# Two-layer conditioned attention: the queries' exponentials of layer 1 taken head by head on ScalarE

## The chip, the cores and the metric

The kernel runs on one core of a Trainium2 chip. The metric is the device time of one execution in microseconds; the time before is the median of three runs. The profile is of one further execution on the same kind of core.

## The reference

Input is `x` of 32 sequences x 128 positions x 512 features, float32, and a condition vector of 1024 values per sequence. Two layers follow each other; each adds its result to its input.

Layer 0 has 16 heads of 32 features and ordinary softmax attention over the positions. Layer 1 has 8 heads of 64 features and linear attention, and the change is in it:

```
xn  = layer_norm(x)
q   = softmax(xn @ Wq + bq, over the 64 features of each head)
k   = softmax(xn @ Wk + bk + (1 - mask) * -1e6, over the 128 positions)
v   = (xn @ Wv + bv) * mask
att = k^T v            (64 x 64 per head)
y   = q att
h   = silu(layer_norm(y) * (1 + scale) + shift) @ W_out + b_out
out = x + h            (scale, shift: from silu(condition) @ W_emb + b_emb)
```

The softmax of the queries needs, for each position and head, the maximum over 64 features, the exponentials of the differences, and the inverse of their sum. The inverse is multiplied in later, when `y` is read.

## The kernel before

Everything is written by hand: five engine programs (PE, DVE, ACT, POOL, and SP for the DMAs) with a semaphore for each kind of operation. Each engine carries out its own list strictly in order, and waits where an operand or a buffer is not ready. A matrix product in float32 precision is made of three products of split operands (`three`, lines 1268 to 1270), hence the tiles `_hi` and `_lo`.

The 32 sequences are worked on in 16 pairs (`GROUP = 2`), and both layers go through `program` (line 254), a software pipeline. One call of `step1(n, f, k, late, slot)` handles three pairs at once: `n` is loaded, normalised and turned; `f` is projected to queries, keys and values; `k` is finished (attention, second normalisation, silu, output product); `late` is the second sequence of the pair before, whose output product and store come last. In full steps `k` runs from pair 0 to pair 13. In the step of pair 14 there is no `n`, in that of pair 15 neither `n` nor `f`. Between the second and the third call stands `film()`, which makes scale and shift from the condition. `b` is 0 or 1, the sequence in the pair.

The lists of layer 1 around the change, each in the engine's order:

- DVE (`step1`, line 1109): output(late,1), kv_out(k,0), key softmax, y_norm(k,0), kv_out(k,1), key softmax, v_add(f,0), y_norm(k,1), the statistics of `n`, film_scale(k,0), q_add(f,0), q_soft(f,0), silu(k,0), v_add(f,1), s_low_part(k,0), film_scale(k,1), k_sums(f), silu(k,1), q_add(f,1), s_low_part(k,1), q_soft(f,1), xt_low(n,0), xt_low(n,1), output(k,0), q_sums(f,0), q_sums(f,1).
- ACT (`step1`, line 770): kt_out(k,0), qt_out(k,0), kt_out(k,1), k_bias and k_exps, qt_out(k,1), k_bias and k_exps, tanh(k,0), q_exps(f,0), s_high(k,0), tanh(k,1), s_high(k,1), xt_high(n,0), xt_high(n,1), q_exps(f,1).
- POOL: residual(k,0), norm2(k,0), v_mask(f,0), norm2(k,1), add_shift(k,0), norm1(n,0), norm1(n,1) (these write `xn`), add_shift(k,1), v_mask(f,1), residual(k,1).
- PE (`step1`, line 1435): turn_k(k,0), turn_q(k,0), turn_k(k,1), output(late,1), key projection, turn_q(k,1), keys_values(k,0), key projection, query(k,0), keys_values(k,1), values, query(k,1), query projection, turn_yn(k,0), values, turn_yn(k,1), query projection, turn(n,0), output(k,0), turn(n,1). `claim` (line 1253) makes PE wait until the last reader of a PSUM bank has finished.

The second half of a sequence is one chain: film_scale (DVE, L981, writes `z_a`), add_shift (POOL, L537, `z_s`), tanh (ACT, L689, `th`), silu (DVE, L988, `th`), s_high (ACT, L694), s_low_part (DVE, L994), output (PE), output (DVE, L1000).

The queries: q_add (L1031) adds the bias into `q_tmp` (shown as `room` in the profile), one buffer for both sequences; q_soft takes the maximum of each head (L1036) and subtracts it into `q_exp` (L1040, also `room`); q_exps (L715) takes all 512 exponentials of a position in one instruction; q_sums adds up each head (L1047) and inverts (L1051) into `q_rec`. In `film()` of layer 1 the sums of the first pair are made.

Of the kernel before, what the change touches and what calls it, by code (L numbers as in the profile page):

```python
# [33 lines left out]
ALU = mybir.AluOpType  # L34
ACT = mybir.ActivationFunctionType
AX = mybir.AxisListType

P = 128
GROUP = 2
# [28 lines left out]
def done(stage, at):  # L68


    if at.reg is None and at.const < 0:
        return stage.always
    return stage.sem, (at + (1 + stage.earlier)).value()
# [10 lines left out]
def upto(stage, value):  # L84

    return stage.sem, stage.earlier + value


def build(nc, t, out):
# [9 lines left out]
             b=[t["L0_cond_q_b"], t["L0_cond_k_b"], t["L0_cond_v_b"], t["L0_cond_out_b"]],  # L99
# [4 lines left out]
             b=[t["L1_cond_bq"], t["L1_cond_bk"], t["L1_cond_bv"], t["L1_cond_b_out"]],  # L104
# [3 lines left out]
    H0, H1 = layers[0]["H"], layers[1]["H"]  # L108
    DH0, DH1 = D // H0, D // H1
# [6 lines left out]
    with ExitStack() as ctx:  # L116
        def sb(name, shape, dt=F32):
            return ctx.enter_context(nc.sbuf_tensor(name, shape, dt))
# [72 lines left out]
        q_exp = room[:, 0, :].rearrange("p (s b d) -> p s b d", s=2, b=GROUP)  # L191
        k_tmp = room[:, 2, 0:2 * D].rearrange("p (s d) -> p s d", s=2)
        q_tmp = room[:, 2, 2 * D:3 * D]
# [7 lines left out]
        q_max = sb("q_max", [P, H1])  # L201
        q_sum = sb("q_sum", [P, H1])
# [13 lines left out]
        def stages(names, earlier=0):  # L216
            return {n: Stage(sem(n), earlier) for n in names.split()}

        def counted_on(these, earlier):
# [15 lines left out]
                 "rec pt_pe0 pt_pe1 pt_pe2 pt_pe3 pt_out0 pt_out1 pt_out2 pt_out3 pv "  # L235
                 "pv_out")
        only1 = ("kt_pe qt_pe kt_out qt_out att_pe att_out kbias0 kbias1 kmax0 kmax1 ksub0 ksub1 kexp0 kexp1 ksum0 ksum1 krec "
                 "q_pe q_add qmax qsub qexp qsum qrec")
        both = stages(STAGES)

        moved = {n: [sem(f"{n}{b}") for b in range(GROUP)] for n in ("x_in_full", "res_in", "stored", "mask_row_in")}
# [349 lines left out]
        def _(act):  # L591
            act.wait_ge(consts, 1)
            for l, L in enumerate(layers):
                s, bk = S[l], BANKS[l]
# [115 lines left out]
                    act.activation(v, v, ACT.Exp).then_inc(s[f"kexp{pair}"].sem, GROUP)  # L710

                def q_exps(f, slot, b):
                    act.wait_ge(*done(s["qsub"], f + b))
                    v = q_exp[:, slot, b, :]
                    act.activation(v, v, ACT.Exp).then_inc(s["qexp"].sem, 1)  # L715

                def kt_out(k, b):
                    act.wait_ge(*done(s["kt_pe"], k + b))
# [86 lines left out]
        def _(dve):  # L805
            dve.wait_ge(consts, 1)
            for l, L in enumerate(layers):
                s, bk = S[l], BANKS[l]
# [83 lines left out]
                def film():  # L892

                    dve.wait_ge(*upto(s["emb_pe"], KE))
                    dve.tensor_tensor(yn[0:2 * B, 0, :], bank[bk["EMB"]][0:2 * B, :], x_out[0:2 * B, 0, :], ALU.add
                                      ).then_inc(s["emb_dve"].sem, 1)
                    dve.tensor_copy(yn[2 * B:4 * B, 0, :], bank[bk["EMB"]][2 * B:4 * B, :]).then_inc(s["emb_dve"].sem, 1)
                    if l == 1:
                        q_sums(At(None, 0), 0, 0)
                        q_sums(At(None, 0), 0, 1)  # L900
                    dve.wait_ge(*upto(s["film_pe"], 1))
                    et = z_s[:].rearrange("p a n -> p (a n)")[:, 0:2 * C * B].rearrange("p (c b) -> p c b", b=B)
                    fd = s["film_dve"]
                    dve.tensor_copy(et.rearrange("p c b -> p (c b)"), bank[bk["FILM"]][:, 0:2 * C * B]).then_inc(fd.sem, 1)
                    dve.wait_ge(*upto(fd, 1))
                    wide = lambda i: col[:, i, :].rearrange("p (c o) -> p c o", o=1).broadcast_to([P, C, B])
                    dve.scalar_tensor_tensor(out=film_a[:], in0=et[:, 0:C, :], scalar=1.0, in1=wide(W2),
                                             op0=ALU.add, op1=ALU.mult).then_inc(fd.sem, 1)
                    dve.scalar_tensor_tensor(out=film_b[:], in0=et[:, 0:C, :], scalar=1.0, in1=wide(B2),
                                             op0=ALU.add, op1=ALU.mult).then_inc(fd.sem, 1)  # L910
                    dve.wait_ge(*upto(fd, 3))
                    dve.tensor_tensor(film_b[:], film_b[:], et[:, C:2 * C, :], ALU.add).then_inc(fd.sem, 1)
                    dve.wait_ge(*upto(fd, 4))
                    if l == 1:
                        dve.wait_ge(*upto(s["zeroed"], 1))
# [81 lines left out]
                def output(at, b):  # L997
                    dve.wait_ge(*done(s["o_pe"], at))
                    dve.wait_ge(*done(s["res_full"], at))
                    dve.tensor_tensor(x_out[:, b, :], bank[bk["O"][b]][:], x_res[:, b, :], ALU.add  # L1000
                                      ).then_inc(s["o_out"].sem, 1)
# [25 lines left out]

                def q_add(f, b):
                    dve.wait_ge(*done(s["q_pe"], f + b))
                    dve.wait_ge(*done(s["qsub"], f + (b - 1)))  # L1030
                    dve.tensor_tensor(q_tmp, bank[bk["Q"][b]][:], bias_wide[:, WQ, :], ALU.add).then_inc(s["q_add"].sem, 1)  # L1031

                def q_soft(f, slot, b):
                    dve.wait_ge(*done(s["q_add"], f + b))
                    qv = q_tmp.rearrange("p (h e) -> p h e", h=H1)
                    dve.tensor_reduce(q_max[:], qv, AX.X, ALU.max).then_inc(s["qmax"].sem, 1)  # L1036
                    dve.wait_ge(*done(s["qmax"], f + b))
                    dve.wait_ge(*done(s["qt_pe"], f + (b - 2 * GROUP)))
                    dve.wait_ge(*done(s["qsum"], f + (b - 2 * GROUP)))
                    dve.tensor_tensor(q_exp[:, slot, b, :].rearrange("p (h e) -> p h e", h=H1), qv,  # L1040
                                      q_max[:].rearrange("p (h o) -> p h o", o=1).broadcast_to([P, H1, DH1]),
                                      ALU.subtract).then_inc(s["qsub"].sem, 1)

                def q_sums(f, slot, b):
                    dve.wait_ge(*done(s["qexp"], f + b))
                    dve.wait_ge(*done(s["qrec"], f + (b - 1)))
                    dve.tensor_reduce(q_sum[:], q_exp[:, slot, b, :].rearrange("p (h e) -> p h e", h=H1), AX.X, ALU.add  # L1047
                                      ).then_inc(s["qsum"].sem, 1)
                    dve.wait_ge(*done(s["qsum"], f + b))
                    dve.wait_ge(*done(s["y_norm"], f + (b - 2 * GROUP)))  # L1050
                    dve.reciprocal(q_rec[:, slot, b, :], q_sum[:]).then_inc(s["qrec"].sem, 1)  # L1051

# [56 lines left out]
                def step1(n, f, k, late, slot):  # L1109
                    if late:  # L1110
                        output(late, 1)
                    if k:
                        kv_out(k, 1 - slot, 0)
                    if f:
                        k_soft(f, slot, 0)
                    if k:
                        y_norm(k, 1 - slot, 0)
                        kv_out(k, 1 - slot, 1)
                    if f:
                        k_soft(f, slot, 1)  # L1120
                        v_add(f, slot, 0)
                    if k:
                        y_norm(k, 1 - slot, 1)
                    if n:
                        stats1(n, 0)
                        stats1(n, 1)
                        if not f:
                            low_parts(1, (2,))
                    if k:
                        film_scale(k, 0)  # L1130
                    if f:
                        q_add(f, 0)
                        q_soft(f, slot, 0)
                    if k:
                        silu(k, 0)
                    if f:
                        v_add(f, slot, 1)
                    if k:
                        s_low_part(k, 0)
                        film_scale(k, 1)  # L1140
                    if f:
                        k_sums(f, slot)
                    if k:
                        silu(k, 1)
                    if f:
                        q_add(f, 1)
                    if k:
                        s_low_part(k, 1)
                    if f:
                        q_soft(f, slot, 1)  # L1150
                    if n:
                        xt_low(n, 1 - slot, 0)
                        xt_low(n, 1 - slot, 1)
                    if k:
                        output(k, 0)
                    if f and k:
                        q_sums(f, slot, 0)
                        q_sums(f, slot, 1)

                def spread_norm_b(l):  # L1160

# [339 lines left out]
```

## Time and profile before

| | |
|---|---|
| median of three runs | 1174.09 us (1173.89 to 1174.12) |
| the profiled execution, its own time | 1175.47 us |
| span of the profiled execution | 1173.5 us |
| PE busy | 1091.3 us (93%) |
| DVE busy | 807.6 us (69%) |
| ACT busy | 556.8 us (47%) |
| POOL busy | 469.7 us (40%) |
| granted TensorE clock, mean | 0.979 |

The busy shares are averages over both layers. Layer 1 begins near 640 us of the span. ACT is much busier in layer 0, where it takes the exponentials of the full attention. In every timeline row below the first number is the start in microseconds from the beginning of the span, the second the duration; what stands in brackets is idle time of that engine just before, and what ended it.

### The profile page before, as it was taken

To read this page: it belongs to the slowest core of one execution; us is meant where nothing else is said; L and a number is where in the kernel's file an instruction comes from. 1 tells how busy PE (TensorE), PEld (TensorE's weight loads), DVE (VectorE), ACT (ScalarE), POOL (GpSimd) and SP (SyncE) were. 2 spreads that over 40 slices of the span, in tenths; PEclk is the share of its full clock that TensorE was granted. 3 is DMA by queue.
4 is the path that set the end of the run, shared out by engine and by line. 5 is a ranking of instruction groups with operands and counts; after the bars stand their busy time and mean duration, and the time that the engine had idled before them with its cause. 6 is when DMAs were issued, how large, how long until landed. Compare 5 with 4: busy or idle time off the path is not lost.

```text
span 1173.5 us, 25383 instructions
## 1 busy us (share of the span) xinstructions
PE 1091.3 (93%) x8426; PEld 929.7 (79%) x8426; DVE 807.6 (69%) x1393; ACT 556.8 (47%) x1726; POOL 469.7 (40%) x783
## 2 busy tenths in 40 slices
PE   5989999999999999999767999999999999999995
PEld 2788888888888888888654788888888888888884
DVE  4357766666776666776546587788777777787774
ACT  3267666787666678766661222223323332223221
POOL 3123344434333443433322245544444445455532
PEclk9989999999999999999979899999999999999998
DMA  7301111011111101120244301111111111101111
GB/s 249 144 22 60 49 50 56 22 58 58 58 46 50 56 22 58 58 60 25 81 135 149 109 9 46 55 54 54 54 54 54 54 54 53 35 34 38 54 37 54
DMA packets 44767, 72.40 MB, mean 62 GB/s; under 512 B 8624, under 2 KB 12816, under 8 KB 44720
## 3 DMA queue, kind: packets, MB, share of 16 engines
q1 hardware_dynamic: 44720, 71.80, 18.8%
q8 instruction: 26, 0.43, 0.2%
q14 instruction: 21, 0.17, 0.0%
HBM read 54.97 MB, written 16.79 MB: 61 GB/s over the span
## 4 chain that ended last, share of the span: by engine, by line
PE 66%; DVE 11%; POOL 9%; issue 7%; ACT 4%; POOLq 1%; DVEq 0%; DMA 0%; ACTq 0%; SPq 0%
PE bank L1268 16%; PE bank L1269 15%; PE bank L1270 15%; PE bank L1321 4%; DVE stat L919 3%; PE bank L1311 3%; PE bank L1334 3%; POOL stat L502 3%; DVE y_s L972 2%; POOL z_s L537 2%; PE bank L1263 1%; ACT room L678 1%; PE bank L1392 1%; DVE s_lo L994 1%; POOL stat L500 1%
## 5 line engine op out<-in xcount | busy, mean ns | idle before, releaser
L1268 PE MATMUL bank<-xt_hi,w_hi 128*128 128x256 f32 x768 | 226.1, 294 | 0.4 <-DVEq L880 0.4
L1269 PE MATMUL bank<-xt_lo,w_hi 128*128 128x256 f32 x768 | 216.5, 282 | 0.0
L1270 PE MATMUL bank<-xt_hi,w_lo 128*128 128x256 f32 x768 | 215.9, 281 | 0.0
L670 ACT ACTIVATE prob<-prob,neg_max 128x128 f32<-128x128 f32 x512 | 198.5, 395 | 12.9 <-DVE neg_max L947 12.8
L499 POOL TENSOR_SCALAR stat<-stat 128x1 f32<-128x1 f32 x128 | 34.5, 269 | 370.1 <-DVE stat L923 357.7
L689 ACT ACTIVATE th<-z_s 128x512 f32<-128x512 f32 x64 | 40.3, 630 | 272.8 <-POOL z_s L537 272.8
L1268 PE MATMUL bank<-w_hi,xt_hi 128*128 128x512 f32 x384 | 158.4, 413 | 0.0
L542 POOL TENSOR_TENSOR x_res<-x_res,bias_wide 128x512 f32<-128x512 f32 x64 | 90.5, 1414 | 161.2 <-DMA x_res<-between_layers 150.0
L1270 PE MATMUL bank<-w_hi,xt_lo 128*128 128x512 f32 x384 | 151.6, 395 | 0.0
L1269 PE MATMUL bank<-w_lo,xt_hi 128*128 128x512 f32 x384 | 151.6, 395 | 0.0
L1268 PEld LDWEIGHTS bank<-xt_hi,w_hi 128*128 128x128 f32 x768 | 147.0, 191 | 3.6 <-issue 1.1
L1269 PEld LDWEIGHTS bank<-xt_lo,w_hi 128*128 128x128 f32 x768 | 146.5, 191 | 0.0
L1270 PEld LDWEIGHTS bank<-xt_hi,w_lo 128*128 128x128 f32 x768 | 146.1, 190 | 0.0
L1268 PE MATMUL bank<-w_hi,s_hi 128*128 128x512 f32 x256 | 108.8, 425 | 16.5 <-DVE s_lo L994 15.6
L1269 PE MATMUL bank<-w_lo,s_hi 128*128 128x512 f32 x256 | 103.1, 403 | 0.0
L1270 PE MATMUL bank<-w_hi,s_lo 128*128 128x512 f32 x256 | 102.6, 401 | 0.0
L670 ACT ACTIVATION_READ_ACCUMULATOR prob<-prob,neg_max 128x1 f32 x512 | 99.4, 194 | 0.0
L944 DVE TENSOR_TENSOR prob<-bank,mask_row 128x512 f32<-128x512 f32 x128 | 87.6, 684 | 15.8 <-PE bank L1311 14.8
L988 DVE SCALAR_TENSOR_TENSOR th<-th,z_s 128x512 f32<-128x512 f32 x64 | 47.0, 734 | 68.7 <-ACT th L689 68.5
L947 DVE TENSOR_REDUCE neg_max<-prob 128x4 f32<-128x512 f32 x128 | 87.8, 686 | 4.4
L537 POOL TENSOR_TENSOR z_s<-z_a,film_b 128x512 f32<-128x512 f32 x64 | 67.1, 1049 | 57.7 <-DVE z_a L981 57.7
L678 ACT ACTIVATE room<-bank 128x512 f32<-128x512 f32 x128 | 74.2, 592 | 30.3 <-PE bank L1321 29.5
(117 smaller groups left out, 2274.3 us busy)
## 6 DMA issues: line engine op xcount, KB each, us to landing
x_in<-in_x_dram SPq DMA_DIRECT2D x32, 256.0 KB, 2.7
x_res<-in_x_dram SPq DMA_DIRECT2D x32, 256.0 KB, 2.8
between_layers<-x_res SPq DMA_DIRECT2D x32, 256.0 KB, 2.0
x_in<-between_layers SPq DMA_DIRECT2D x32, 256.0 KB, 2.8
x_res<-between_layers SPq DMA_DIRECT2D x32, 256.0 KB, 3.0
out_dram<-x_res SPq DMA_DIRECT2D x32, 256.0 KB, 2.9
prob<-in_L_cond_emb_w_dram SPq DMA_DIRECT2D x8, 512.0 KB, 7.5
prob<-in_L_cond_W_emb_dram SPq DMA_DIRECT2D x8, 512.0 KB, 6.6
```

The source lines that it names most:

```text
L537: pool.tensor_tensor(chunks(z_s[:, b, :]), chunks(z_a[:]), film_of(film_b, k + b), ALU.add).then_inc(s["z_full"].sem, 1)
L542: pool.tensor_tensor(x_res[:, b, :], x_res[:, b, :], bias_wide[:, WO, :], ALU.add).then_inc(s["res_full"].sem, 1)
L670: last = act.activation(prob[:, b, i, :], prob[:, b, i, :], ACT.Exp, bias=neg_max[:, b, i:i + 1], accum_out=row_sum[:, b, h:h + 1])
L678: act.activation(prob_t[:, g, :], bank[bk["PT"][g % 2]][:], ACT.Copy).then_inc(s[f"pt_out{g}"].sem, 1)
L689: act.activation(th[:], z_s[:, b, :], ACT.Tanh, scale=0.5).then_inc(s["tanh_full"].sem, 1)
L944: dve.tensor_tensor(prob[:, b, heads, :], bank[c][:].rearrange("p (r n) -> p r n", r=HC0), row, ALU.add).then_inc(s[f"masked{c}"].sem, 1)
L947: dve.tensor_reduce(neg_max[:, b, heads], prob[:, b, heads, :], AX.X, ALU.max, negate=True).then_inc(s[f"neg{c}"].sem, 1)
L988: dve.scalar_tensor_tensor(out=s_s[:], in0=th[:], scalar=1.0, in1=z_s[:, b, :], op0=ALU.add, op1=ALU.mult).then_inc(s["s_full"].sem, 1)
L1268: pe.matmul(o, hi, w_h, start=first, stop=False)
L1269: pe.matmul(o, hi, w_l, start=False, stop=False)
L1270: return pe.matmul(o, lo, w_h, start=False, stop=stop)
L1321: last = pe.transpose(bank[bk["PT"][g % 2]][:, c * P:(c + 1) * P], prob[:, b, C * g + c, :], ident[:])
```

## The change

The maximum of a head is now taken negated. ACT reads the biased queries directly and takes the exponentials of each head of 64 features in an instruction of its own, with the negated maximum as the bias and with the sum of the head as its accumulator output. DVE's subtraction and DVE's sums are gone; the reciprocal alone stays, as `q_inverse`. For b=0 it moves to a place between silu(k,1) and q_add(f,1); for b=1 it stays at the end of the step. q_add now waits for the exponentials of the sequence before, since these read `q_tmp`. The exponentials wait for the maximum, for the free `q_exp` buffer and for the inverse of the sequence before.

```
 def q_exps(f, slot, b):
-    act.wait_ge(*done(s["qsub"], f + b))
-    v = q_exp[:, slot, b, :]
-    act.activation(v, v, ACT.Exp).then_inc(s["qexp"].sem, 1)
+    act.wait_ge(*done(s["qmax"], f + b))
+    act.wait_ge(*done(s["qt_pe"], f + (b - 2 * GROUP)))
+    act.wait_ge(*done(s["qrec"], f + (b - 1)))
+    for h in range(H1):
+        head = slice(h * DH1, (h + 1) * DH1)
+        last = act.activation(q_exp[:, slot, b, head], q_tmp[:, head], ACT.Exp, bias=q_max[:, h:h + 1],
+                              accum_out=q_sum[:, h:h + 1])
+    last.then_inc(s["qexp"].sem, 1)
...
 # film(), layer 1
-    q_sums(At(None, 0), 0, 0)
-    q_sums(At(None, 0), 0, 1)
+    q_inverse(At(None, 0), 0, 1)
...
 def q_add(f, b):
     dve.wait_ge(*done(s["q_pe"], f + b))
-    dve.wait_ge(*done(s["qsub"], f + (b - 1)))
+    dve.wait_ge(*done(s["qexp"], f + (b - 1)))
...
 def q_soft(f, slot, b):
     dve.wait_ge(*done(s["q_add"], f + b))
-    dve.tensor_reduce(q_max[:], qv, AX.X, ALU.max).then_inc(s["qmax"].sem, 1)
-    (waits) dve.tensor_tensor(q_exp..., qv, q_max..., ALU.subtract).then_inc(s["qsub"].sem, 1)
+    dve.tensor_reduce(q_max[:], q_tmp.rearrange("p (h e) -> p h e", h=H1), AX.X, ALU.max, negate=True
+                      ).then_inc(s["qmax"].sem, 1)
-def q_sums(f, slot, b):
+def q_inverse(f, slot, b):
     dve.wait_ge(*done(s["qexp"], f + b))
-    (wait) dve.tensor_reduce(q_sum[:], q_exp..., AX.X, ALU.add).then_inc(s["qsum"].sem, 1)
     dve.wait_ge(*done(s["y_norm"], f + (b - 2 * GROUP)))
     dve.reciprocal(q_rec[:, slot, b, :], q_sum[:]).then_inc(s["qrec"].sem, 1)
...
 # step1 of DVE
     if f:
+        q_inverse(f, slot, 0)
         q_add(f, 1)
...
     if f and k:
-        q_sums(f, slot, 0)
-        q_sums(f, slot, 1)
+        q_inverse(f, slot, 1)
```

## Rows read from the trace of the kernel before

**Rows 1.** Stretch, its length, busy us per engine (instructions), clock, DMA share, GB/s.
```profile
883.30:915.20 31.90, 30.65 (x190) 26.21 (x189) 24.68 (x43) 9.50 (x18) 15.75 (x25) 1.00 0.16 49
```

**Rows 2.** Chain that ended last, 866 to 892 us: start, duration, what.
```profile
879.24 0.70 DVE z_a L981
...
886.57 1.06 POOL z_s L537
...
888.32 0.87 DVE th L988
...
889.88 1.01 DVE s_lo L994
...
891.02 0.47 PE bank L1268
```

**Rows 3.** Groups of instructions, layer 1, DVE: busy us, mean ns, idle before.
```profile
L1047 DVE TENSOR_REDUCE q_sum<-room 128x8 f32<-128x512 f32 x32 | 21.8, 681 | 1.7
```

**Rows 4.** Timeline of ACT, layer 1: tanh(k,0) and s_high(k,0).
```profile
881.19 0.63 ACT L689 ACTIVATE th<-z_s 128x512 f32<-128x512 f32 x1 [5.43 <-POOL z_s L537]
...
882.61 0.64 ACT L694 ACTIVATE s_hi<-th 128x512 fp32r<-128x512 f32 x1
```

**Rows 5.** Timeline of ACT, layer 0: a tanh and two exponentials with sums.
```profile
304.96 0.63 ACT L689 ACTIVATE th<-z_s 128x512 f32<-128x512 f32 x1 [7.42 <-POOL z_s L537]
305.50 0.39 ACT L670 ACTIVATE prob<-prob,neg_max 128x128 f32<-128x128 f32 x1
305.79 0.18 ACT L670 ACTIVATION_READ_ACCUMULATOR prob<-prob,neg_max 128x1 f32 x1
305.89 0.39 ACT L670 ACTIVATE prob<-prob,neg_max 128x128 f32<-128x128 f32 x1
```

**Rows 6.** Groups of instructions, ACT, 0 to 600 us, a wide one.
```profile
L622 ACT ACTIVATE w_hi<-v_s 128x1024 fp32r<-128x1024 f32 x1 | 1.0, 1045 | 0.0
```

**Rows 7.** Timeline of DVE, one step of layer 1.
```profile
883.28 0.73 DVE L994 TENSOR_TENSOR s_lo<-th,s_hi 128x512 fp32r<-128x512 f32 x1
883.93 0.68 DVE L981 TENSOR_TENSOR z_a<-bank,film_a 128x512 f32<-128x512 f32 x1
...
886.00 0.20 DVE L1025 RECIPROCAL k_rec<-k_sum 128x8 f32<-128x8 f32 x1 [0.20 <-DVE k_sum L1019]
...
889.10 0.68 DVE L1031 TENSOR_TENSOR room<-bank,bias_wide 128x512 f32<-128x512 f32 x1
```

**Rows 8.** Timeline of PE, the same step: output(k,0) and turn_k(k,1).
```profile
884.96 0.48 PE L1268 MATMUL bank<-w_hi,s_hi 128*128 128x512 f32 x1
...
889.84 0.66 PE L1368 MATMUL bank<-ident,q_t 128*128 128x128 f32 x4 [0.53 <-DVE room L1031]
```

**Rows 9.** Timeline of POOL, the same step: the two first normalisations.
```profile
883.21 1.28 POOL L508 TENSOR_SCALAR xn<-x_in,stat 128x512 f32<-128x512 f32 x1 [0.21 <-POOL stat L502]
...
885.84 0.77 POOL L508 TENSOR_SCALAR xn<-x_in,stat 128x512 f32<-128x512 f32 x1 [0.21 <-POOL stat L502]
```

**Rows 10.** Timelines of ACT and PE, the step before: k_bias(f,0) and turn_q(k,1).
```profile
865.27 0.84 ACT L703 ACTIVATE room<-bank,col 128x256 f32<-128x256 f32 x2 [2.84 <-PE bank L1270]
...
865.07 0.60 PE L1375 MATMUL bank<-ident,room 128*128 128x128 f32 x4
```

**Rows 11.** Timelines of DVE and PE at the start of layer 1.
```profile
660.51 0.69 DVE L1040 TENSOR_TENSOR room<-room,q_max 128x512 f32<-128x512 f32 x1
...
663.86 3.22 PE L1244 MATMUL bank<-pick,yn 128*128 128x32 f32 x16 [2.11 <-DVE yn L897]
```

**Rows 12.** Timelines of POOL, ACT, DVE and PE, the step of pair 14.
```profile
1139.19 1.05 POOL L537 TENSOR_TENSOR z_s<-z_a,film_b 128x512 f32<-128x512 f32 x1 [3.46 <-DVE z_a L981]
...
1137.15 0.63 ACT L694 ACTIVATE s_hi<-th 128x512 fp32r<-128x512 f32 x1 [0.21 <-DVE th L988]
...
1143.43 0.67 DVE L1036 TENSOR_REDUCE q_max<-room 128x8 f32<-128x512 f32 x1
...
1147.01 1.15 PE L1383 MATMUL bank<-v_s,prob 128*128 128x128 f32 x8
```

More of the change, by code:

```diff
@@ L237, in build @@
         only1 = ("kt_pe qt_pe kt_out qt_out att_pe att_out kbias0 kbias1 kmax0 kmax1 ksub0 ksub1 kexp0 kexp1 ksum0 ksum1 krec "
-                 "q_pe q_add qmax qsub qexp qsum qrec")
+                 "q_pe q_add qmax qexp qrec")
         both = stages(STAGES)
@@ L1034, in q_soft @@
                     dve.wait_ge(*done(s["q_add"], f + b))
-                    qv = q_tmp.rearrange("p (h e) -> p h e", h=H1)
-                    dve.tensor_reduce(q_max[:], qv, AX.X, ALU.max).then_inc(s["qmax"].sem, 1)
[L1037 to L1042, printed above, removed]
-                def q_sums(f, slot, b):
+                    dve.tensor_reduce(q_max[:], q_tmp.rearrange("p (h e) -> p h e", h=H1), AX.X, ALU.max, negate=True
+                                      ).then_inc(s["qmax"].sem, 1)
+                def q_inverse(f, slot, b):
                     dve.wait_ge(*done(s["qexp"], f + b))
[L1046 to L1049, printed above, removed]
                     dve.wait_ge(*done(s["y_norm"], f + (b - 2 * GROUP)))
```

## The prediction

> **What bounds the kernel now.** I read the busy shares by stretch first. In layer 1 one step (a pair of sequences) takes 31.9 us, of which PE is busy 30.65, DVE 24.7, ACT 9.5 and POOL 15.8 [rows 1]. So PE is nearly full and ACT nearly empty, but PE's remaining 1.25 us of idle time per step are what a change on the vector or scalar side can move. Next comes the chain that ended last [rows 2]: DVE scales the first sequence (film_scale(k,0), 879.24), POOL then works through its queue, and its add_shift(k,1) starts at 886.57; from there the chain runs without slack through tanh, silu (888.32) and s_low(k,1) (889.88 to 890.88) to PE's output product at 891.02, where PE had been idle 0.53 us. The period is that loop, not PE's sum alone. The timelines of each engine then say which of the changed instructions lie on this loop.
>
> **What goes.** DVE loses, per sequence, one subtraction (0.69 us [rows 11]) and one sum (681 ns on average [rows 3]): 2 x 1.37 = 2.75 us per step. The subtraction of b=0 ended just before silu(k,0), which waits for tanh(k,0) anyway (tanh ends at 881.19 + 0.63 = 881.82 [rows 4]): nothing. The subtraction of b=1 and both sums come after s_low(k,1), when PE has its operand; DVE then runs into waits for PE of about 2 us before the next step's work. In steady state I price all DVE savings at 0. If that cover were gone, the most they could give is 2.75 us per step, which PE's 1.25 us of idle time caps.
>
> **What is added.** ACT replaces one exponential of 512 columns (0.63 us, like the tanh of the same width [rows 4]; the next instruction starts 0.54 to 0.60 later) by 8 of 64 columns, each followed by an accumulator read. The trace has this pair at 128 columns: exponential 0.39, read 0.18, start to start 305.50 to 305.89, a pitch of 0.385 us [rows 5]. Width: 1024 columns take 1.045 us [rows 6], 512 take 0.63 [rows 4], so 0.81 ns a column; 64 columns fewer save 0.052. Pitch 0.333 us, 8 of them 2.66 us. Bounds: 0.285 below (three spacings of the 0.095 between a read and the next exponential), and 0.57 above (0.39 + 0.18, no overlap); the likely upper end is 0.385, no shortening at all. I take 0.333, because the row is the same form and only narrower.
>
> **Where the 2.66 us land, first sequence.** The exponentials stand between tanh(k,0) and s_high(k,0) on ACT. A step's exponentials can follow tanh 0.54 us after its start, as in [rows 5], so they run from 881.73 to 884.39, and s_high(k,0) starts at 884.4 instead of 882.61 [rows 4]: 1.8 us late. Queued behind it are tanh(k,1) and s_high(k,1). On DVE, s_low(k,0) waits for it, and behind that film_scale(k,1), the key sums and silu(k,1). s_low(k,0) goes from 883.28 to 885.07, film_scale(k,1) from 883.93 to about 885.72 [rows 7].
> - PE's output(k,0) started at 884.96 [rows 8]; now s_low(k,0) is done at 885.77 and PE starts 0.14 later, 885.9: 0.95 us of new idle time. But PE idled 0.53 at 889.84 and 0.53 at 891.02 [rows 8, 2]; these absorb it: PE would reach the output product at about 890.7, still ahead of 891.02. Price 0.
> - POOL's add_shift(k,1) needs film_scale(k,1): 885.72 + 0.69 + 0.17 = 886.57, exactly when POOL takes it now. Until now it was bound by POOL's own queue, two normalisations before it; now it is bound by the ACT detour, in a dead heat. Price 0 (the sum gives 886.55 against 886.57).
> - silu(k,1) at 888.32: DVE's work before it, whose last instruction was done at 886.2 [rows 7], is now done at 888.0. Free by 0.3 us.
> - The new reciprocal of b=0 stands between silu(k,1) and q_add(f,1): it pushes q_add by some 0.13, from 889.10 to 889.23 [rows 7]. s_low(k,1) was waiting for s_high(k,1) until 889.88, and the adder's successor can start 0.61 later, 889.84. Price 0, at most 0.13.
>
> **Port collisions.** xn(1), POOL's second normalisation, took 0.77 us while DVE did a reduction; xn(0) at 883.21 took 1.28 while DVE's s_low ran, an operation with two SBUF inputs [rows 9, 7]. Now s_low(k,0) at 885.07 falls where xn(1) runs (885.84 before, about 884.6 to 885.5 now, since xn(0) is undisturbed). A DVE operation that meets a running POOL one is stretched: s_low(k,1) took 1.00 against 0.73 [rows 7, 2]. That is 0 to 0.27 per step on film_scale(k,1). I take half: 0.13.
> The Trainium skill (SBUF — State Buffer, section "Who interferes with whom") says that a DVE instruction with two SBUF inputs and a GpSimd instruction that reads SBUF exclude each other and the first to start wins. The rows agree in kind; by this rule, should POOL start first each time, the full 0.27 or more would be paid, which is a rival below.
>
> Steady state: -0.02 + 0.13 = about +0.12 us a step, over the 14 steps that have a following load, a projection and a finishing pair (pairs 0 to 13): +1.7 us.
>
> **Second sequence.** Its exponentials follow the two xt_high copies. In a normal step they start 0.74 us earlier than the one exponential did, because the subtraction is gone, and last 2.66 instead of 0.54; the three copies behind them (kt_out, qt_out, kt_out) move by 2.66 - 0.54 - 0.74 = 1.4 us. ACT stood idle for 2.84 us after these copies, until 865.27, and PE takes turn_q(k,1), the first to need one, at 865.07 [rows 10]. Price 0, slack 1.2 us or more. DVE's last reciprocal waits for these exponentials, and behind it is output(late,1), whose product PE has ready no earlier. Price 0.
>
> **Start.** Before the conditioning stage DVE is on the path: maximum, subtraction (660.51), two xt_low, two copies, then PE's small products at 663.86 after 2.11 us of idle time [rows 11]. The subtraction leaves: 0.61 at most; the copies also wait for the embedding products, which end near 661.75, so I take -0.5. The two sums of that stage lay beside PE's 3.2 us: 0.
>
> **End.** Pair 14 has no following normalisation. There POOL waited 3.46 us for film_scale(k,1) and started at 1139.19 [rows 12]: nothing covers the detour. s_high(k,0) moves 1137.15 to 1138.96, and the whole chain by 1.8, so that the maximum of the second sequence starts at 1145.24 instead of 1143.43 [rows 12] and ends at 1145.9, its exponentials at 1148.6; qt_out starts after kt_out, 1149.1, and ends at 1149.7. PE's turn_q(k,1) must find that bank emptied, and takes 0.5; keys_values, at 1147.01 before [rows 12], then starts at 1150.1. There is no projection left for PE to fill the time with, and everything to the end hangs on it: +3.1 us (1.8 if only the first detour counted).
>
> **Sum.** -0.5 + 1.7 + 3.1 = +4.3 us. The profiled execution took 1175.47 us (span 1173.5 and 2.0 around it), 1.4 above the median of 1174.09; it would become 1179.8, and the median 1178.4.
>
> **Rivals.**
> - Longer pitch. If 64 columns cost as much as 128 (0.385), film_scale(k,1) is late by 8 x 0.052 = 0.42 more a step, since the dead heat leaves nothing to absorb it: 14 x 0.42 + 0.8 at the end = +6.7, 1185. Without overlap (0.57) it is 8 x 0.237 = 1.9 a step, some +30: 1208. For: three waits stand ahead of the first exponential. Against: [rows 5] has the overlap and hidden waits. 0.16 together.
> - Full collision: POOL's xn(1) first every time, +0.27 to 0.5 a step, 14 x 0.25 above my term: 1182. 0.11.
> - Faster, by one mechanism: POOL's queue. Without the subtraction and with s_low(k,0) moved away, POOL's normalisations end up to 1.1 us earlier and add_shift(k,1) could start at 885.5. That decides only if the pitch is below 0.333, because film_scale(k,1) holds it otherwise. At 0.285, add_shift starts 0.40 early: -5.6, with -0.5 and an end of +2.3: 1170.3. 0.10.
> - The change is nearly hidden: no collision and only the first detour counted at the end: -0.5 - 0.3 + 1.8 = +1.0, 1175.1. 0.17.
> - My case, 0.46: 1178.4, its own range 1176.6 to 1181.
>
> A measurement of this kernel can tell about 0.2% (2.3 us) from no change. Slower by more: 0.46 + 0.16 + 0.11 = 0.73; within it 0.17; faster 0.10. The range leaves out the far ends of the first and third rival: 1172.0 to 1186.0.
>
> **What would show it.** The profile after should have exponentials of 64 columns at a pitch near 0.33, DVE's busy time down by 32 x 1.38 = 44 us, ACT's up by 32 x (8 x (0.34 + 0.19) - 0.63) = 115 us, a wait of PE's output(k,0) for s_low near 0.9 us in each step, waits of turn_k(k,1) for q_add gone, and add_shift(k,1) released by DVE instead of by POOL's own queue. The period of film_scale(k,0) should be 32.0 instead of 31.9. I am wrong if the period falls (the POOL queue was the true limit and ACT is quick enough), or if it rises by 0.4 or more (pitch or collision), or if keys_values of the last pair is not late by about 3 us.

## The result, and the profile after

The changed kernel takes 1178.53 us (median of 6, 1178.02 to 1180.34) against 1174.11 us (6 runs, 1171.51 to 1174.53): a ratio of 1.0043, 95% interval 1.003 to 1.0056. It is slower by 4.4 us; 1178.4 was forecast, with a range of 1172 to 1186.

The profiled execution has a span of 1176.8 us. DVE's busy time fell from 807.6 to 761.5 us, ACT's rose from 556.8 to 621.8. Below are, of the page and of the busy time by stretch, the busy line and one full step [rows 1].

```profile
PE 1088.4 (92%) x8426; PEld 931.0 (79%) x8426; DVE 761.5 (65%) x1329; ACT 621.8 (53%) x2206; POOL 451.8 (38%) x783
```

```profile
883.50:915.53 32.03, 30.42 (x188) 26.30 (x188) 22.40 (x39) 13.54 (x48) 14.11 (x25) 1.00 0.16 49
```

A step lasts 32.03 us instead of 31.90; DVE has 2.3 us less to do in it and ACT 4.0 more. The groups of ACT in layer 1 show the new instructions (busy us, mean ns, idle before).

```profile
L718 ACT ACTIVATE room<-room,q_max 128x64 f32<-128x64 f32 x256 | 85.3, 334 | 17.4 <-DVE q_max L1039 17.4
L718 ACT ACTIVATION_READ_ACCUMULATOR room<-room,q_max 128x1 f32 x256 | 47.9, 187 | 0.0
```

Next the timeline of ACT in a full step, from tanh(k,0) to tanh(k,1) [rows 4, 5].

```profile
879.64 0.63 ACT L689 ACTIVATE th<-z_s 128x512 f32<-128x512 f32 x1 [5.43 <-POOL z_s L537]
880.18 0.34 ACT L718 ACTIVATE room<-room,q_max 128x64 f32<-128x64 f32 x1
880.42 0.19 ACT L718 ACTIVATION_READ_ACCUMULATOR room<-room,q_max 128x1 f32 x1
880.51 0.33 ACT L718 ACTIVATE room<-room,q_max 128x64 f32<-128x64 f32 x1
...
882.84 0.61 ACT L694 ACTIVATE s_hi<-th 128x512 fp32r<-128x512 f32 x1
886.24 0.63 ACT L689 ACTIVATE th<-z_s 128x512 f32<-128x512 f32 x1 [2.78 <-POOL z_s L537]
```

From one exponential to the next is 0.333 us, the pitch (880.18 to 882.84 is eight of them). Behind them, at 882.84, s_high(k,0) starts, 3.20 us after tanh(k,0) started, against 1.42 before. Timeline of DVE, the same step [rows 7].

```profile
883.48 0.90 DVE L998 TENSOR_TENSOR s_lo<-th,s_hi 128x512 fp32r<-128x512 f32 x1 [1.88 <-ACT s_hi L694]
884.30 0.68 DVE L985 TENSOR_TENSOR z_a<-bank,film_a 128x512 f32<-128x512 f32 x1
...
886.90 0.86 DVE L992 SCALAR_TENSOR_TENSOR th<-th,z_s 128x512 f32<-128x512 f32 x1 [0.33 <-ACT th L689]
887.69 0.19 DVE L1045 RECIPROCAL q_rec<-q_sum 128x8 f32<-128x8 f32 x1
887.80 0.63 DVE L1035 TENSOR_TENSOR room<-bank,bias_wide 128x512 f32<-128x512 f32 x1
888.47 1.00 DVE L998 TENSOR_TENSOR s_lo<-th,s_hi 128x512 fp32r<-128x512 f32 x1
```

Timeline of POOL [rows 9], and of PE [rows 8], the same step.

```profile
878.56 1.05 POOL L537 TENSOR_TENSOR z_s<-z_a,film_b 128x512 f32<-128x512 f32 x1 [0.50 <-DVE z_a L985]
...
880.96 0.77 POOL L508 TENSOR_SCALAR xn<-x_in,stat 128x512 f32<-128x512 f32 x1 [0.21 <-POOL stat L502]
...
883.08 0.77 POOL L508 TENSOR_SCALAR xn<-x_in,stat 128x512 f32<-128x512 f32 x1 [0.21 <-POOL stat L502]
885.15 1.05 POOL L537 TENSOR_TENSOR z_s<-z_a,film_b 128x512 f32<-128x512 f32 x1 [1.30 <-DVE z_a L985]
```

```profile
884.53 0.47 PE L1262 MATMUL bank<-w_hi,s_hi 128*128 128x512 f32 x1 [1.27 <-DVE s_lo L998]
...
889.61 0.48 PE L1262 MATMUL bank<-w_hi,s_hi 128*128 128x512 f32 x1 [0.31 <-DVE s_lo L998]
```

POOL, which used to reach add_shift(k,1) straight from its own queue [rows 2], now stands idle for 1.30 us until film_scale(k,1) is done. add_shift(k,1) starts 6.59 us after add_shift(k,0); it was 6.47. PE's wait has moved from turn_k(k,1) to output(k,0).

Both traces split at the same instructions give this ledger. A second trace of the kernel before, taken later, stands beside the first.

The parts are named by the instruction that ends them; "the end" is the last DVE operation, and the span ends 2.5 us behind it in each trace.

| part of layer 1 | before | before, again | after | after - before | predicted |
|---|---|---|---|---|---|
| to q_add(0,1) | 659.06 | 658.17 | 657.28 | -1.78 | - |
| to the first film_scale | 28.64 | 28.64 | 28.16 | -0.48 | -0.5 |
| 13 periods of film_scale(k,0) | 13 x 31.905 | 13 x 31.947 | 13 x 32.040 | +1.75 | +1.6 |
| to film_scale(14,0) | 31.00 | 31.07 | 30.98 | -0.02 | +0.1 |
| to keys_values(15,0) | 13.54 | 13.55 | 16.71 | +3.17 | +3.1 |
| to film_scale(15,0) | 9.12 | 9.12 | 9.13 | +0.01 | 0 |
| to the end | 14.89 | 14.88 | 15.55 | +0.66 | 0 |

The four parts behind the first, where changed instructions act, add up to +4.4 us. The third of them is the forecast's fourteenth step; it did not lengthen. Against the second trace of the kernel before, the 13 periods are longer by 1.2 us instead of 1.75, so this row is known to half a microsecond only. The first and last rows also differ between executions of one kernel or of kernels that are alike there. q_add(0,1) waits for PE in every trace, and the first row was 656.4 to 659.1 over all the traces below. The last was 14.87 to 14.89 in nine traces of thirteen; here the granted TensorE clock was 0.50 from 1160 to 1166 us and 0.69 in the 8.3 us behind that, against 0.71 and 0.80 in the same stretches of the kernel before.

### The profile page after: what moved, and what is told of

It is laid out like the page before. It is cut to its first block, busy times and chain, and to the rows that moved or that the text cites. A ratio compares the mean times of both kernels' runs of the same rounds, so it can differ in the third digit from the quotient of the medians.

```text
span 1176.8 us, 25767 instructions
## 1 busy us (share of the span) xinstructions
PE 1088.4 (92%) x8426; PEld 931.0 (79%) x8426; DVE 761.5 (65%) x1329; ACT 621.8 (53%) x2206; POOL 451.8 (38%) x783
## 4 chain that ended last, share of the span: by engine, by line
PE 64%; DVE 13%; ACT 9%; POOL 7%; issue 6%; DVEq 1%; POOLq 0%; DMA 0%; ACTq 0%; SPq 0%
PE bank L1262 16%; PE bank L1263 15%; PE bank L1264 14%; PE bank L1315 4%; DVE stat L923 3%; ACT room L718 3%; PE bank L1305 3%; PE bank L1328 3%; POOL z_s L537 3%; DVE y_s L976 2%; DVE z_a L985 2%; ACT s_hi L694 2%; PE bank L1257 2%; ACT room L678 1%; DVE s_lo L998 1%
## 5 line engine op out<-in xcount | busy, mean ns | idle before, releaser
L1262 PEld LDWEIGHTS bank<-w_hi,s_hi 128*128 128x128 f32 x256 | 49.5, 193 | 57.4 <-issue 46.5
L718 ACT ACTIVATE room<-room,q_max 128x64 f32<-128x64 f32 x256 | 85.3, 334 | 17.4 <-DVE q_max L1039 17.4
```

Of the source, the lines that this page charges most:

```text
L718: last = act.activation(q_exp[:, slot, b, head], q_tmp[:, head], ACT.Exp, bias=q_max[:, h:h + 1], accum_out=q_sum[:, h:h + 1])
L1262: pe.matmul(o, hi, w_h, start=first, stop=False)
```

## The experiments

Each was timed against the kernel before on the same chip; experiments 5, 10 and 11 ran on another chip than the rest, so kernels are compared by their ratios. In the edits, "..." stands for lines left out, and the declarations of spare tiles are not shown. "Step" is the mean of 13 periods of film_scale(k,0) in its trace.

**1. The first sequence's exponentials behind s_high(k,0).**

```
                     if k:
                         tanh(k, 0)
+                        s_high(k, 0)
                     if f:
                         q_exps(f, slot, 0)
                     if k:
-                        s_high(k, 0)
                         tanh(k, 1)
```

> The eight exponentials of the first sequence stand behind s_high(k,0) instead of ahead of it on ACT; all else is the changed kernel. Theory: in the changed kernel they delay s_high(k,0), s_low(k,0), film_scale(k,1) and add_shift(k,1), which POOL could have started 1.30 us earlier. Moved, film_scale is ready about 2 us earlier and POOL's own queue binds again, some 5.9 us after add_shift(k,0) instead of 6.59, so a step takes about 31.4 us instead of 32.03: 14 x 0.65 = 9 us, and 1.8 us at pair 14. Time about 1168, between 1163 and 1172. Rival (the exponentials' place is irrelevant, the period is POOL's queue or PE's sum): within 2 us of the changed kernel, 1177 to 1180. Second rival: q_add(f,1), which now waits for later exponentials, delays s_low(k,1) and the time rises above 1180.

Measured: 1163.6 us, ratio 0.9907 (0.9892 to 0.9922), step 31.13. This beats both kernels. The theory named the right place and direction and undersized the gain: POOL's queue lets add_shift(k,1) start after 5.69 us, not 5.9, and the trace also has the shorter of the two starts of layer 1 (26.76 us instead of 28.16), which is not the move's doing. The timeline of POOL in a step shows what is left.

```profile
841.59 1.05 POOL L537 TENSOR_TENSOR z_s<-z_a,film_b 128x512 f32<-128x512 f32 x1 [0.52 <-DVE z_a L985]
...
843.99 0.78 POOL L508 TENSOR_SCALAR xn<-x_in,stat 128x512 f32<-128x512 f32 x1 [0.21 <-POOL stat L502]
844.84 0.66 POOL L499 TENSOR_SCALAR stat<-stat 128x1 f32<-128x1 f32 x1
...
847.28 1.05 POOL L537 TENSOR_TENSOR z_s<-z_a,film_b 128x512 f32<-128x512 f32 x1
```

add_shift(k,1) waits for nothing but POOL's queue. xn(0) takes 0.78 us instead of 1.28 [rows 9]. One delay is left in that queue: the small operation at 844.84, started 0.12 us after s_low(k,0), takes 0.66 us, and 0.23 in the step of the changed kernel.

**2. In the last pair, the copies ahead of the exponentials.**

```
                         kt_out(k, 1)
+                    if k and not f:
+                        q_exps(k, 1 - slot, 1)
...
-                    if f:
+                    if f and (n or not k):
                         q_exps(f, slot, 1)
```

> In the last pair alone, ACT does the copies kt_out, qt_out, kt_out ahead of the eight exponentials of the second sequence. Theory: these copies cost PE 1.05 us at turn_q(k,1) after the exponentials; now only the exponentials remain (ready at 1148.05 instead of a bank emptied at 1149.1). Time 1.0 us below the changed kernel: 1177.5. Rival (the end hangs on the first sequence's detour of 1.8 us and on the output chain alone): no difference, 1178.5.

Measured: 1177.58 us, ratio 1.0026 (1.0017 to 1.0035), as forecast; but this interval overlaps that of the changed kernel, and it is the trace that decides. In it keys_values(15,0) comes 15.82 us after film_scale(14,0) instead of 16.71, the 0.9 us that the theory asked for, with the step unchanged at 32.06.

**3. Both moves.** The two edits above together.

> Both moves together. Theory: their gains add up, since one acts in the full steps and the other after them: about 1167, that is 1 us below the first. Rival: once the first sequence's detour is gone the second's exponentials are early enough and the second move adds nothing.

Measured: 1163.6 us, ratio 0.9909 (0.9895 to 0.9922), the same as with the first alone. The times cannot decide it: the second gain is 1 us, and either interval is 3 us wide. In the traces the gains add up: from film_scale(14,0) to the last DVE operation 38.69 us with both moves and 39.67 with the first alone. keys_values(15,0) comes 0.9 us earlier (14.07 against 14.95). Of this 0.6 is lost before film_scale(15,0) (9.74 against 9.13 us), and 0.7 comes back behind it (14.88 against 15.58). The granted clock goes with it. The first of these two stretches, with both moves:

```profile
1133.40:1143.10 9.70, 5.74 (x38) 5.02 (x36) 4.90 (x11) 0.60 (x1) 3.04 (x5) 0.83 0.27 82
```

Its clock is 0.83; with the first move alone it was 0.93 (1134.8 to 1143.9 us). Behind it the order is the other way, 0.65 with both and 0.60 with the first alone. This is one trace of each.

**4. A ninth exponential in the first sequence.**

```
+                    if b == 0:
+                        act.activation(spare[:], q_tmp[:, 0:DH1], ACT.Exp, bias=q_max[:, 0:1], accum_out=spare_sum[:])
                     for h in range(H1):
```

> The changed kernel with a ninth exponential of 64 columns with a sum, into a spare tile, ahead of the eight of the first sequence. Theory (ACT's detour is on the loop with no slack): +0.333 us in each of 14 steps and once at the end, 15 x 0.333 = +5.0 us: 1183.5. Rival (POOL's queue or PE holds the period, ACT's detour is covered): less than +1 us, 1178.5 to 1179.5.

Measured: 1179.99 us, ratio 1.0049 (1.0036 to 1.0063), step 32.16: 0.12 us a step, a third of the forecast. The time alone could not be told from that of the changed kernel; the step can, since the traces of four kernels that share its step (the changed one, experiments 2, 6 and 7) have it at 32.04 to 32.06. The theory failed as it was put. The timelines of DVE and POOL around s_low(k,0) say why.

```profile
850.39 0.69 DVE L1002 TENSOR_TENSOR s_lo<-th,s_hi 128x512 fp32r<-128x512 f32 x1 [2.21 <-ACT s_hi L696]
851.00 0.68 DVE L989 TENSOR_TENSOR z_a<-bank,film_a 128x512 f32<-128x512 f32 x1
```

```profile
849.65 0.77 POOL L510 TENSOR_SCALAR xn<-x_in,stat 128x512 f32<-128x512 f32 x1 [0.21 <-POOL stat L504]
```

With nine, xn(1) ends at 850.42, just when s_low(k,0) starts, and s_low takes 0.69. With eight it started at 883.48 while xn(1) ran until 883.85, and took 0.90. The ninth costs its 0.33 and gives 0.21 back. That is the collision of the forecast, with its size: it was being paid in every full step (s_low(k,0) takes 0.89 to 0.91 us for pairs 0 to 13, and 0.69 for pair 14, which has no xn).

**5. A tenth.** The line for the ninth once more, with a spare tile of its own.

> The changed kernel with two more exponentials of 64 columns with sums ahead of the eight of the first sequence. The ninth cost 0.12 us a step, not the 0.33 of its pitch, because it also moved s_low(k,0) (0.90 to 0.69 us) behind POOL's xn(1), which had slowed it. Theory: that relief is spent, so the tenth costs its full pitch: step 32.16 to 32.49 us, time 5.0 us above that of nine: 1185.0. Rival (ACT's detour is only partly on the loop): another 0.12 us a step, 1181.5.

Measured: 1186.73 us, ratio 1.0109 (1.0094 to 1.0125), 6.7 us above nine. Eleven of the 13 periods in its trace lie at 32.34 to 32.57, mostly 32.5, 0.33 above those of nine (mostly 32.2). Past the collision, ACT's detour passes into the step in full. Two periods are 33.5 and lift the mean to 32.65. In both the granted TensorE clock fell to its lower level (1.2 of 2.4 GHz) for some 3.5 us, just after PE had waited for s_low(k,0) and begun output(k,0). No other full step of layer 1 in the thirteen traces has such a fall. The stretch by busy time, and PE around its start:

```profile
790.90:794.50 3.60, 3.60 (x12) 2.78 (x11) 3.03 (x6) 1.75 (x3) 2.98 (x4) 0.53 0.00 0
```

```profile
789.69 0.47 PE L1269 MATMUL bank<-w_hi,s_hi 128*128 128x512 f32 x1 [1.84 <-DVE s_lo L1005]
...
791.67 0.63 PE L1270 MATMUL bank<-w_lo,s_hi 128*128 128x512 f32 x1
```

Products of 0.39 us take 0.63 there. The second fall is at 855.8 us, behind a wait of 1.82. So in the trace about 2 us of the 6.7 go with the clock; the rest is the tenth exponential, near the 5.0 of the theory.

**6. The second sequence in one exponential.**

```
-                    for h in range(H1):
-                        head = slice(h * DH1, (h + 1) * DH1)
+                    for h in range(1 if b else H1):
+                        head = slice(h * DH1, (h + 1) * DH1) if b == 0 else slice(0, D)
```

> The changed kernel, but the second sequence's exponentials are one instruction of 512 columns with the first head's maximum and one sum; left out: the other seven heads' own maxima and sums of the second sequences. Theory: in full steps the second sequence's detour is covered, so the step stays at 32.04 us; only at the last pair turn_q(k,1) waits for it, and 2.66 - 0.75 = 1.9 us come back there: 1176.7. Rival (ACT's total work, or the late reciprocal ahead of output(late,1) on DVE, is part of the loop): the step falls too, below 1174.

Measured: 1176.68 us, ratio 1.0022 (1.0013 to 1.0032), which just overlaps the changed kernel's interval. Step 32.06; keys_values(15,0) after 15.28 us instead of 16.71, 1.4 of the 1.9 us that the theory asked for. The second sequence's eight exponentials are free in the steps and cost at the end alone.

**7. DVE's saved work put back as idle work.**

```
+                    if b == 1:
+                        dve.wait_ge(*done(s["qmax"], f + b))
+                        dve.tensor_tensor(spare[:]..., q_tmp..., q_max[:]..., ALU.add)
...
                     if f and k:
+                        idle_sums(f, slot)    # two tensor_reduce of q_exp into a spare tile
                         q_inverse(f, slot, 1)
```

> The changed kernel with idle DVE work where the kernel before had its own: a 512-column operation behind the second maximum, and two sums of 512 columns at the end of the step, results unused: 2.0 us of DVE work a step. Theory: it lies in DVE's waits for PE, 0 in the steps and at most 0.5 at the last pair: 1178.5 to 1179. Rival (DVE's saved work carries part of the result): up to 2.0 us a step, anything above 1183.

Measured: 1180.53 us (1178.33 to 1180.9), ratio 1.0041 (1.0027 to 1.0055), where the changed kernel had 1.0043. Step 32.06, keys_values(15,0) after 16.71 as before. The 2.0 us of DVE work a step are worth nothing. The stretch to the first film_scale is back at 28.64 us, from 28.16: the 0.48 us of the ledger are this one subtraction (more on this stretch under "The start" below).

**8. Experiment 1 with the first sequence's subtraction back, as idle work.**

```
+                    if b == 0:
+                        dve.wait_ge(*done(s["qmax"], f + b))
+                        dve.tensor_tensor(spare[:]..., q_tmp..., q_max[:]..., ALU.add)
```

> The kernel with the exponentials moved behind s_high(k,0) (1163.6 us, step 31.13 us), plus one idle DVE operation with the queries and the broadcast maxima as its two SBUF inputs, where the first sequence's subtraction used to be. Theory: the 0.78 us a step that the move gains over the kernel before come from the missing subtraction: with it, POOL's small operations and xn(0) start 0.3 us late and then meet silu and s_low(k,0). With it back, the step returns to 31.7 to 31.9 us and the time to 1171.5 to 1174.5. Rival (the gain is from something else, such as shorter waits on ACT): the step stays at 31.13 and the time at 1163 to 1165.

Measured: 1175.71 us, ratio 1.0011 (1.0002 to 1.002), step 31.91, that of the kernel before (31.905 and 31.947). The time lies 1.2 us above the theory's range, the step at its upper end; the exponentials still lengthen the end (keys_values(15,0) after 14.92 us against 13.54). Timelines of DVE and POOL.

```profile
845.31 0.69 DVE L1044 TENSOR_TENSOR spare<-room,q_max 128x512 f32<-128x512 f32 x1
845.93 0.68 DVE L993 SCALAR_TENSOR_TENSOR th<-th,z_s 128x512 f32<-128x512 f32 x1
...
847.31 0.73 DVE L999 TENSOR_TENSOR s_lo<-th,s_hi 128x512 fp32r<-128x512 f32 x1
```

```profile
845.59 0.49 POOL L501 TENSOR_SCALAR stat<-stat 128x1 f32<-128x1 f32 x1
846.04 0.99 POOL L503 TENSOR_TENSOR stat<-stat,minus_half 128x1 f32<-128x1 f32 x1
847.24 1.28 POOL L509 TENSOR_SCALAR xn<-x_in,stat 128x512 f32<-128x512 f32 x1 [0.21 <-POOL stat L503]
```

Without the operation at 845.31 these three POOL instructions take 0.22, 0.57 and 0.78 us. DVE's own time is not what it costs: it holds POOL up, and POOL's delay then meets silu and s_low(k,0). The whole 0.78 us a step by which experiment 1 beats the kernel before is this.

**9. POOL's add_shift(k,1) ahead of norm1(n,1), with both moves on ACT.**

```
                             norm1(n, 0)
-                            norm1(n, 1)
                         if k:
                             add_shift(k, 1)
+                        if n:
+                            norm1(n, 1)
```

> Both moves, and POOL's add_shift(k,1) ahead of its second normalisation norm1(n,1) instead of behind it. Theory: add_shift(k,1) now waits for POOL's queue, though film_scale(k,1) is ready 1.2 us earlier; ahead of the normalisation it and the chain to s_low(k,1) come up to 1.2 us earlier, until PE, idle 0.8 us a step, is full: step 30.4 to 30.6 us, 14 x 0.6 = 8 us, 1155 to 1157. Rival: xn(1) is now ready 1.2 us later and PE waits for it at turn(n,1) instead: 1162 to 1166.

Measured: 1156.17 us, ratio 0.9837 (0.9822 to 0.9851), step 30.62. A step by busy time shows PE full.

```profile
883.50:914.08 30.58, 30.12 (x190) 26.09 (x189) 21.47 (x39) 13.70 (x48) 14.03 (x24) 1.00 0.16 53
```

**10. The same order of POOL in the kernel before, and nothing else.** The edit of experiment 9.

> The kernel before, unchanged but for POOL's order: add_shift(k,1) ahead of norm1(n,1). Theory: the limit of the kernel before is POOL's queue; film_scale(k,1) is ready 2 us before POOL takes it. PE, busy 30.65 us a step, becomes the limit, with some 0.5 us of waits for xn(0) and xn(1), since the subtraction still makes xn(0) late: step 31.1 to 31.2 us, 1174.2 - 14 x 0.75 = 1163.7. The same order with the exponentials on ACT took 1156.2; the difference of 7 us would be what the missing subtraction gives. Rival (the order alone does it all): 1156 to 1158 as well.

Measured: 1156.13 us, ratio 0.9845 (0.9832 to 0.9859), step 30.65. My theory fell and its rival held: this order alone does it all. Its step and its PE.

```profile
883.50:914.10 30.60, 30.30 (x190) 26.04 (x190) 25.09 (x44) 9.62 (x18) 15.73 (x24) 1.00 0.16 51
```

```profile
844.18 0.65 PE L1264 MATMUL bank<-ident,xn 128*128 128x128 f32 x4 [0.29 <-POOL xn L508]
```

xn(0) is still slow here (1.32 us), and PE's one wait left is the 0.29 us for it above; in experiment 9 PE waits 0.46 us for xn(1) instead. PE is busy 30.30 us in 30.60, so what experiment 9 saves on DVE and POOL has nowhere to go (experiment 9 had both moves on ACT; this order with the exponentials where the changed kernel has them was not run). I had added 0.5 us of waits to the 30.65 of [rows 1]; the waits come to 0.3, and the busy time itself is lower in the shorter step.

**11. The kernel before, once more.** No edit.

> The kernel before once more, for a second trace. Theory: the 1.8 us by which the changed kernel's trace is ahead at its first layer-1 bias addition of the second query projection (657.28 against 659.06), before any changed instruction has had an effect, is variation between executions: this time falls within 656.3 to 659.1 here too. Rival: the kernel before is always later there, at 659.

Measured: 1175.51 us for this one execution, the second column of the ledger. q_add(0,1) starts at 658.17, inside the interval; all thirteen traces, in each of which PE releases it, spread over 656.4 to 659.1. So the 1.8 us by which the changed kernel's trace is ahead there are variation.

## Why the prediction was right, point by point

- **The bound.** The loop from add_shift(k,0) through POOL's queue to s_low(k,1) held the period, and not PE's sum: shown by experiment 10, where one change of POOL's order takes 1.3 us off each step, and by experiment 9, where it takes 0.5 off what the moves on ACT had left.
- **DVE's savings at 0.** Right for the second sequence's subtraction and both sums (experiment 7). Wrong in the reasoning for the first sequence's subtraction, which was put at nothing because silu waits for tanh. Its absence frees POOL by 0.78 us a step (experiment 8). That it gave nothing in this kernel because the ACT detour held film_scale(k,1) back is read from POOL's idle 1.30 us; no run put this subtraction back into the changed kernel itself. The rival of POOL's queue had this mechanism, but I gave it 0.10 and tied it to a shorter pitch, not to a better place of the exponentials.
- **The pitch.** 0.333 us forecast from exponentials of 128 columns, 0.333 measured; the bounds of 0.285 and 0.57 were not needed.
- **The detour.** s_high(k,0) was to start 3.20 us after tanh(k,0), and does. add_shift(k,1) was to come 6.45 us after add_shift(k,0) plus half a collision; it comes 6.59 after. The collision is 0.21 and in every step, not 0.13 on average; the row that I built on already had 0.04 of it (s_low(k,0) at 0.73 [rows 7] against 0.69 undisturbed), and s_high is 0.03 shorter than before. The sum, +0.12 forecast and +0.09 to +0.14 measured (by which trace of the kernel before is taken), came out right through small errors of opposite sign; that is luck. The term of -0.02 in it is a slip: 885.72 + 0.69 + 0.17 gives 886.58, and not the 886.55 that I compared with 886.57. The dead heat is one between the detour and the time at which POOL used to be free. In the changed kernel the detour holds add_shift(k,1) alone, with POOL idle for 1.30 us: one more exponential costs, a move of them gains 0.9 us a step.
- **The rule on the shared port.** The Trainium skill (SBUF — State Buffer, section "Who interferes with whom") lets the first to start win and block the other. Experiments 4 and 8 agree on who waits where one starts well inside the other: s_low(k,0), starting 0.40 us into xn(1), is longer by 0.21 us; POOL's two operations started under the idle subtraction and silu (845.59, 846.04) are longer by 0.27 and 0.42. Full blocking by the recorded times would have given 0.37, 0.41 and 0.57. Each is short of that by about the same 0.15 us, and so are s_low(k,1) before (0.31 longer, with 0.45 us left of POOL's addition to x_res, 888.61 to 890.33) and the operation at 844.84 of experiment 1 (0.43 of 0.58). That fits a full block whose holder lets go 0.15 us before its recorded end; that it does so is an inference, since POOL's recorded times are rough. Over the thirteen traces, from 680 us on, all 536 POOL operations that start with 0.17 us or more left of a DVE operation with two SBUF inputs are longer than the shortest of their kind by over 0.08 us, and none of the 1609 that start so under another DVE operation is. Where the starts lie close together the recorded order does not tell who waits: xn(0) at 847.24 is recorded 0.07 us ahead of s_low(k,0), and it is the one that grows, by 0.50 us, s_low by 0.04.
- **PE.** The wait at output(k,0) was put at 0.95 us and is 1.27, since xn(0) is no longer late (PE had waited for it before) and s_low is longer. The wait at turn_k(k,1) is gone as forecast. Neither is on the loop, since PE still waits 0.31 us for s_low(k,1).
- **silu(k,1) and the moved reciprocal.** 0.3 us of slack forecast, 0.33 measured; q_add(f,1) at 887.80 does not delay s_low(k,1), which starts 3.32 us after add_shift(k,1), against 3.31.
- **The second sequence.** Free in the steps, as forecast (experiment 6). ACT's idle time after the three copies went from 2.84 to 1.46 us, the 1.4 of the forecast.
- **The start.** -0.5 forecast, -0.48 in the ledger, and experiment 7 gives it back. But of the nine traces without this subtraction only four have 28.14 to 28.17 us here; the other five have 26.70 to 26.76, and all four traces with it have 28.64 to 28.66. So the stretch is shorter by 0.5 or by 1.9 us, with the granted clock (see the last section), and the prediction knew of the first alone.
- **Busy time.** DVE's was to fall by 44 us and fell by 46.1. ACT's was to rise by 115 us and rose by 65.0: I added up the durations of exponentials and reads, 0.53 us a pair, though they overlap and a pair takes the pitch of 0.333. 32 x (8 x 0.333 - 0.63) is 65. The forecast of the time used the pitch and is untouched.
- **The end.** +3.1 forecast, +3.17 measured. The timelines of ACT and PE after [rows 12] show the chain as it was put: exponentials from 1145.38, copies from 1148.05, then turn_q(k,1).

```profile
1145.38 0.35 ACT L718 ACTIVATE room<-room,q_max 128x64 f32<-128x64 f32 x1 [1.66 <-DVE q_max L1039]
...
1148.05 0.57 ACT L725 ACTIVATE prob<-bank 128x512 f32<-128x512 f32 x1
1148.53 0.58 ACT L730 ACTIVATE prob<-bank 128x512 f32<-128x512 f32 x1
```

```profile
1149.15 0.66 PE L1369 MATMUL bank<-ident,room 128*128 128x128 f32 x4 [1.23 <-ACT prob L730]
```

Experiments 2 and 6 take 0.9 and 1.4 us back from this part by two different edits.

The mechanism and its place in the steps and at the end were right. That the whole is right to 0.1 us (+4.4 against +4.3) is partly luck: the interval of the ratio is 3 us wide, the start could have been 1.4 us shorter, and the trace's last row has 0.66 us that go with a lower clock.

What stays open: what decides in a given execution when the granted clock falls. With ten exponentials it fell after waits of 1.84 and 1.82 us, and did not in another step after one of 1.83.

## What to carry to other kernels

An idle engine is not a free engine: ACT was busy 30% of a step, and the work moved to it cost time mostly because of the one place in its list where it was put, between two links of a chain; one place further back the same work made the kernel 1% faster. Before moving work between engines, find the queue in which the longest chain waits though its operand is ready: here that was an addition of POOL behind a normalisation, and exchanging the two gave 1.5% with no other change, after which the moved work, in its better place, was worth nothing. And the price of a DVE operation with two SBUF inputs is to be read on POOL's timeline as well as on DVE's.

## What the runs showed of the hardware that I had not expected

- A DVE operation of 0.69 us slowed POOL by 0.78 us a step in all, more than its own length, because the delay it caused made two later POOL operations meet two later DVE ones (experiment 8).
- Lengthening a path by 0.33 us cost 0.12 (experiment 4), because it moved an operation out of a collision.
- The stretch from q_add(0,1) to the first film_scale took either 28.16 or 26.7 us in traces with the same instructions there. In the slower ones the granted TensorE clock was low for longer: PE's 16 small products (L1238) took 2.76 us in the trace of the changed kernel, with a clock of 0.91 (656 to 664 us) and 0.66 (664 to 672), and 1.94 us in that of experiment 1, with 1.00 and 0.79. PE had waited and run narrow products just before in both; what decides between the two, these runs don't show.
